# Attention in front of a routed FFN: queries loaded two iterations ahead, and another pair of tiles summed by TensorE

## The reference

```python
x = x + xattn(layernorm(x), ctx, ctx)     # x: 4096 x 512, ctx: 3202 x 512
x = x + ffn(layernorm(x))                 # top 2 of 8 experts, 512 -> 512

def xattn(queries, keys, values):         # 16 heads of 32
    q, k, v = queries @ Wq + bq, keys @ Wk + bk, values @ Wv + bv
    A = softmax(q k^T / sqrt(32))         # per head, 4096 x 3202
    return (A v) @ Wo + bo
```

## Time and profile before

| | us |
|---|---|
| median of three runs | 2718.87 (2716.11 to 2719.77) |
| profiled execution | 2717.32 |
| its span, first to last instruction | 2715.5 |
| outside the span | 1.8 |
| TensorE matmul busy | 2550.3 (94%) |
| VectorE busy | 2194.6 (81%) |
| ScalarE busy | 1880.0 (69%) |
| mean granted clock of TensorE | 0.965 |

### The profile page before, as it was taken

How to read it: one execution, slowest core, us unless ns; L and a number is a source line. 1 busy time by engine, 2 the same in 40 slices (tenths; PEclk the granted TensorE clock), 3 DMA queues, 4 the chain that set the end, 5 groups by cost and what they waited for, 6 DMA issues and landing times. The chain is left out here.

```text
span 2715.5 us, 43246 instructions
## 1 busy us (share of the span) xinstructions
PE 2550.3 (94%) x14123; PEld 1323.7 (49%) x14123; DVE 2194.6 (81%) x1810; ACT 1880.0 (69%) x2173; POOL 488.9 (18%) x548
## 2 busy tenths in 40 slices
PE   9999399999999999998999999999999987969998
PEld 7878144334333343343443433334334346858776
DVE  4377499999889999898998998889999975657565
ACT  3123388888788888887887888778888864623433
POOL 2113101001001110010010100100101014415664
PEclk9999699999999999999999999999999998969999
DMA  7445841111151111015111111511111028824373
GB/s 252 159 161 208 195 108 28 44 25 25 25 121 25 29 32 37 25 25 121 25 29 25 36 33 25 108 39 25 29 33 36 25 65 275 291 71 131 125 226 125
DMA packets 132923, 232.05 MB, mean 85 GB/s; under 512 B 23634, under 2 KB 56922, under 8 KB 131940
## 3 DMA queue, kind: packets, MB, share of 16 engines
q1 hardware_dynamic: 110468, 177.57, 23.3%
q0 software_dynamic: 22240, 51.68, 6.2%
HBM read 155.32 MB, written 91.66 MB: 91 GB/s over the span
## 5 line engine op out<-in xcount | busy, mean ns | idle before, releaser
L1021 ACT ACTIVATE probs<-psum 128x1024 f32<-128x1024 f32 x1664 | 1566.7, 1039 | 286.4 <-PE psum L1136 241.1
L1073 DVE TENSOR_TENSOR sums<-sums,probs 128x2048 f32<-128x2048 f32 x704 | 1647.4, 2340 | 109.5 <-ACT probs L1021 86.8
L1136 PE MATMUL psum<-q_st,k_st 97*128 97x512 f32 x3328 | 1003.5, 425 | 81.0 <-ACT probs L1021 36.1
L1136 PEld LDWEIGHTS psum<-q_st,k_st 97*128 97x128 f32 x3328 | 569.8, 190 | 743.4 <-ACT probs L1021 597.5
L1148 PE MATMUL psum<-probs,v_st 128*32 128x512 f32 x6656 | 843.3, 606 | 8.7 <-ACT probs L1021 8.7
L1148 PEld LDWEIGHTS psum<-probs,v_st 128*32 128x32 f32 x6656 | 159.2, 109 | 382.4 <-issue 296.2
L1847 PE MATMUL psum<-we_hi,wo 128*128 x624 | 218.6, 412 | 5.3 <-issue 4.9
L730 POOL DMA_DIRECT2D sum_scratch<-shared_rows x32 | 18.9, 591 | 1075.2 <-ACT shared_rows L987 1074.8
L1700 ACT ACTIVATE wo<-psum 128x512 fp32r<-128x512 f32 x78 | 46.5, 596 | 129.3 <-PE psum L1833 129.2
L1847 PEld LDWEIGHTS psum<-we_hi,wo 128*128 128x128 f32 x624 | 119.2, 191 | 31.3 <-issue 5.9
L1073 DVE TENSOR_TENSOR sums<-probs 128x2048 f32<-128x2048 f32 x32 | 73.4, 2292 | 75.2 <-ACT probs L1021 75.2
(11 more groups left out here) (197 smaller groups left out, 2040.5 us busy)
## 6 DMA issues: line engine op xcount, KB each, us to landing
q_st<-qh_scratch SPq DMA_DIRECT2D x64, 256.0 KB
token_rows<-rows SPq DMA_DIRECT2D x8, 1040.0 KB, 5.2
xn<-in_x SPq DMA_DIRECT2D x16, 512.0 KB, 6.8
qh_scratch<-o_hi SPq DMA_DIRECT2D x8, 1024.0 KB, 4.5
ql_scratch<-o_lo SPq DMA_DIRECT2D x8, 1024.0 KB, 7.8
q_st<-ql_scratch SPq DMA_DIRECT2D x32, 256.0 KB
token_rows<-in_x SPq DMA_DIRECT2D x1, 8192.0 KB, 31.0
shared_rows<-inv_scratch POOLq DMA_DIRECT2D x128, 64.0 KB, 2.2
```

The lines of the kernel that those rows point to most:

```text
L1021: nc.scalar.activation(probs[:, p_slot[t], 2 * half:2 * half + 2, :], psum[:, 2 * slot:2 * slot + 2, :], ACT.Exp, scale=SCALE).then_inc(ex ...
L1073: nc.vector.tensor_tensor(sums[b][:], a[:], probs[:, p_slot[t]], ALU.add).then_inc(added, 1)
L1136: mm = nc.tensor.matmul(psum[:, 2 * slot + h % 2, :], k_st[:, h, t * P:(t + 1) * P], q_st[:, b, h, :], start=True, stop=True)
```

## The change

SyncE's order changes in three places. The queries of iteration 1 are loaded ahead of everything that follows the first keys and values. In `step`, the load of queries moves behind the reload of keys and values, waits for all scores of `it` instead of `it - 1`, and loads iteration `it + 2` into the buffer that `it` has just left. It still stands in front of the wait for the result. `SUM_ON_PE` changes from tiles 24 and 25 to tiles 13 and 25; the count of tiles that each engine sums stays.

```diff
-SUM_ON_PE = (24, 25)
+SUM_ON_PE = (13, 25)
...
-                def step(j, c, b, k, reload, more=True):
+                def step(j, c, b, k, reload, loads=True, stores=True):
                     it = j * NC + c
-                    if more:
-
-                        sp.wait_ge(s_ready, it * NP)
-                        queries(it + 1, 1 - b)
                     if reload:
                         keys_values(j + 1, it)
-                    if more:
+                    if loads:
+
+                        sp.wait_ge(s_ready, (it + 1) * NP)
+                        queries(it + 2, b)
+                    if stores:
                         result(j, it, b, k)
...
                     values(0, None, n)
+                queries(1, 1)
...
-                    step(j, NC - 2, 0, NC // 2 - 1, False)
-                    step(j, NC - 1, 1, NC // 2 - 1, not last, not last)
+                    step(j, NC - 2, 0, NC // 2 - 1, False, not last)
+                    step(j, NC - 1, 1, NC // 2 - 1, not last, not last, not last)
```

## The result

| | before | after |
|---|---|---|
| median of six runs of each, us | 2718.78 (2716.11 to 2720.42) | 2734.81 (2729.45 to 2756.65) |
| ratio | 1 | 1.0071 [1.0038, 1.0104] |
| profiled execution, its span | 2717.32, 2715.5 | 2731.94, 2730.2 |
| mean granted clock in it | 0.965 | 0.962 |

The change makes the kernel 0.7% slower, by more than the 0.2% that can be told from no change, and lies outside the predicted range.

The account below looks back on a forecast made before the run. TensorE was taken to bound the kernel, held up a little by ScalarE through the PSUM slots. Terms -9.7 - 1.5 + 3.8 + 2.4 - 2.0 + 2.0 = -5.0 us against 2717.3 gave 2712.3, stated as 2713; range 2702 to 2729.

Parts of the forecast that it names:

- keys at 8 and 24: Ends of groups: keys leave earlier, ahead of queries; 4.3 us gained at iteration 8, 5.4 at 24, together -9.7.
- iteration 16: Keys' stream further on when ScalarE's code is fetched at its jump; -1.5 us, between 1.2 lost and 4.5 gained.
- iteration 0: Iteration 1's queries stand in front of the output weights, so ScalarE waits longer; +3.8 us, bounds 3 and 7.
- ScalarE's code at eight jumps: At ScalarE's loop jumps outside 16, the second code transfer meets the first queries; 0.3 us each, +2.4.
- tile from 24 to 13: TensorE's ones cost more at 13 in some iterations, less at 24; -2.0 us over attention.
- clock, and the rest of the eight iterations: Clock term: spells at 1.2 GHz around jumps at 7, 13, 19, 25 gained or lost; +2 us, bounds -6.9 and +6.9.
- Rival B: Code fetch at ScalarE's eight jumps waits for queries, 1.3 to 3.4 us each; 2720 to 2737 us; chance 0.20.

Follow-up runs that it names:

- the best version: The change with all loops written out, iteration 1's queries behind the output weights, next group's first keys/values issued earlier and ScalarE's output-weight read later, against before: 2618.75 us, 0.9633.

## Why the prediction was wrong

The terms, by profiled executions, with the iterations above:

| term | predicted | measured |
|---|---|---|
| keys at 8 and 24 | -9.7 | -3.7 - 4.2 = -7.9 |
| iteration 16 | -1.5 | +0.5 |
| iteration 0 | +3.8 | +4.8 |
| ScalarE's code at eight jumps | +2.4 | 8 x 1.39 = +11.1 |
| tile from 24 to 13 | -2.0 | 0 |
| clock, and the rest of the eight iterations | +2.0 | +4.8 |
| start of attention (302.0 to 302.7) | 0 | +0.7 |
| sum | -5.0 | +14.0 (of 14.6) |

**The step that failed** is "I take 0.3 us at eight jumps". What led to it held: queries move from T + 1.90 on (908.85 in iteration 10's terms), in front of the second transfer of code and, at six of the eight jumps, just behind the start of the first. (At 10 and 19 the first started 0.1 and 0.6 us behind them, and these two lost most, 1.8 and 2.0 us.) What the second pays for that was wrong. It came 0.9 to 1.7 us later, 1.24 on average, ScalarE resumed 1.39 us later, and I had set the price near the lower of my two bounds, of nothing and 3.4 us, without a row that spoke for that end. The one row on the matter, the fetch in a full stream at 16, spoke for the other; there I read 5.4 us of harm and then called it a case of its own. Its size is no price for the second transfer either: before the change it is the first that comes late at 16, at T + 6.45 where it is at 1.8 to 2.0 elsewhere, and the second follows 0.95 us behind. What holds the first up there is not shown. The difference, 8.7 us, is the largest single part of the miss, which is 19.6 us by the profiled executions (-5.0 against +14.6). It is not all of it: with 1.39 for 0.3 the sum gives 2721, still inside the range, and the other terms, each short on the same side, make up 10.3 us more. Rival B had the mechanism, and at its lower price, one of the three DMAs of queries or 1.3 us, also the size per jump. As a time that price gives 2720. That the measured 2734.81 lies between B's 2720 and 2737 is luck: the upper end stands for 3.4 us per jump, and what filled the distance were the other terms. That it is the moment of the loads is shown: they alone carry the loss (1.0062); later loads take it away, by 12 halves (1.0001) and in E also by two, though not in the clock; and without the jump the early loads cost nothing (0.9769 against 0.9778).

The Trainium skill (DMA: Bandwidth & Descriptors, section on queues, rings and completion order) has each DMA engine take turns between queues by whole packets of descriptors, from which the prediction had set down 2721. The delay of 0.9 to 1.7 us agrees with it in size. In iteration 16's full stream the two transfers of code stood 0.97 us apart after the change, less than the 1.3 us of one DMA of queries. No run here varies the size of the DMA in front, so that it is a batch of descriptors that the code waits for is not shown.

Two slips stand in the prediction itself. Its sum of 2712.3 with 1.6 for the median makes 2713.9, not 2713, and a range up to 2729 holds about half of B's 2720 to 2737, not most.

**The keys.** Right in mechanism, a little short in size: 24 gave 4.2 of 5.4 us, and a wait of 1.81 us is left there, where I had 0.6; 8 gave 3.7 of 4.3, with a wait of 1.03 us where I had none. TensorE at the starts of the two:

```profile
796.91 1.19 PE L1137 MATMUL psum<-q_st,k_st 97*128 97x512 f32 x4 [1.03 <-DMA k_st<-kl_scratch]
...
1756.33 0.73 PE L1137 MATMUL psum<-q_st,k_st 97*128 97x512 f32 x2 [1.81 <-DMA k_st<-kl_scratch]
```

Both spells at 1.2 GHz went with the wait, as said (mean clock 1.00 in both stretches).

**Iteration 16** gained nothing. ScalarE's code still meets the stream of keys (8.08 us for 7.68): the stream starts earlier, and the fetch finds it full all the same. Of the two ends I gave, it was that of no gain.

**Iteration 0.** The wait for the output weights is 13.65 us, as forecast (13.7). The iteration grew by 1 us more than the wait.

**The tile** changed no undisturbed iteration by over 0.05 us, alone (1.0004) or with the later loads. The two parts of the term, 0.54 us lost beside a single weigh and 0.8 saved in front of a jump, came from rows of other tiles; neither shows. Beside a single weigh, TensorE's wait for ScalarE seems to take the ones in; this I argue from the unchanged lengths, no run looks at it. In front of a jump TensorE idles anyway.

**The clock.** The spells at 1.2 GHz in iterations 1 to 31 add up to 61.4 us after and 44.4 before. They went from 24 and 8 and came at 4, 10 and 28 (3.4, 6.8 and 13.7 us), where none was before; the stretch from 2003.00 above shows one of them, at 0.50. What I had as +2 came to +4.8 with all else in these eight iterations. But in the kernel with only the tile moved, whose jumps are as before, a spell of 13.7 us stands in 28 too. So a single trace doesn't tell which spell the longer gap brings. The mean granted clock over all runs does tell that the change has more of them: 0.9582 on both chips where 0.9645 is usual before. That the longer gaps bring them is not shown: loads later by two halves have E as before and 0.9607. Whether the tile has a share in it stays open too: with the loads alone the mean is 0.9618, but the two ratios, 1.0062 and 1.0064, are alike.

The measured terms lead from 2717.3 to 2731.3, 0.6 us short of the profiled 2731.94; the median of the runs lies 2.9 above that. So the parts were nearly the right ones (only the later start of attention, 0.7 us, had no term). One had the wrong price by 8.7 us, and the smaller misses all lay on the same side as it.

## What to carry to other kernels

A load that is moved to a quiet moment should be checked against all that uses the DMA engines then, and a loop's jump is such a user: code is fetched there, an engine stands still until it comes, and a load that was never waited for becomes costly by 1.4 us per jump. Where a row shows a like collision elsewhere in the kernel, a price near nothing needs a row of its own; but the size doesn't carry over as it is (5.4 us in the full stream, 1.39 here). And where engines work in step for thousands of instructions, writing the loops out is worth a trial before the loads around them are tuned: here ScalarE's loop alone gave 2.2%, both loops with the moved loads 3.2%, and the moved loads at their best without that 0.2%.

## What the runs showed that was not expected

- **A loop costs ScalarE something in every iteration.** Written out, each iteration lost 1.0 to 1.15 us of 56 to 59, far from any jump. The traces show where: exponentials back to back start 0.90 us apart with the loop and without, but behind a wait for scores the next exponential starts sooner. The typical distance from the start of a half's second matmul to its exponential is 0.58 us with the loop and 0.43 without it, at about eleven such waits in an iteration. The idle time in front of a burst of six shows it, in the kernel before and in the same with ScalarE's loop written out:

```profile
1000.41 5.61 ACT L1021 ACTIVATE probs<-psum 128x1024 f32<-128x1024 f32 x6 [0.73 <-PE psum L1136]
...
1001.06 5.61 ACT L1021 ACTIVATE probs<-psum 128x1024 f32<-128x1024 f32 x6 [0.59 <-PE psum L1133]
```

In the loop, register arithmetic for slots and counts stands between exponentials, and written out it is nearly gone (3088 register operations of ScalarE in the trace before, 38 after). Nothing here separates it from other effects of the loop. It also shows that ScalarE's hold on TensorE through the slots is worth more than its 69% of busy time tells.
- **A jump has a price and an echo.** ScalarE idles 2.3 us, and TensorE's own jumps, taken away in the version with all loops written out, gave 3.4 to 3.7 us each (59.8 to 60.1 us down to 56.42), a spell at 1.2 GHz included.
- **Runs spread with the clock.** The first six runs of the change lie 27 us apart, those of before beside them 4 us; but on the other chips the kernel before spreads by 11 to 19 us in 17 to 23 runs, so few runs don't give a spread. Across the runs of one kernel, 0.001 less of mean granted clock goes with some 2 us more (1.2 to 3.1 in all but the best version). Versions with fewer gaps had a higher clock: 0.9676 with ScalarE's loop written out, 0.970 with all, 0.974 in the best.
- **With the early queries, iteration 16 isn't bound to its keys.** With ScalarE's loop written out it takes 56.67 us instead of 66.75. All but the 1.1 us that every iteration gains was code in a full stream, and what followed from it. With the queries where they were before, it takes 62.44, and there TensorE does wait for keys, 2.8 us: the late keys that ScalarE's jump had covered. So the change's gain at 16 was there to be had, behind the jump.
